# Scores of the first attention: four 64-row matmuls a tile become two of 128 rows

## The chip, the cores and the metric

The kernel runs on one core of one Trainium2 chip. The metric is the device time of one execution in microseconds (us); the time before is the median of three executions that were not profiled. In the profile PE is the matmul engine and PEld its weight load, DVE the vector engine, ACT the scalar engine, POOL GpSimd, and SP the engine that issues most of the plain transfers.

## The reference

Two graph attention layers over 12,500 nodes and 200,000 edges sorted by target node, four heads of 64 channels each, every layer followed by layer norms. The change lies in the scores of the first one:

```python
Q = (enh @ Wq + bq).reshape(N, H, D)
K = (enh @ Wk + bk).reshape(N, H, D)
mod_k = K[src] + 0.2 * rel[:, None, :]
scores = jnp.einsum('ehd,ehd->eh', Q[dst], mod_k) / D ** 0.5
seg_max = jax.ops.segment_max(scores, dst, num_segments=N)
ex = jnp.exp(scores - seg_max[dst])
...
agg = jax.ops.segment_sum(w[:, :, None] * V[src], dst, num_segments=N)
```

Everything is float32.

## The kernel before, in words

Four stages follow one another. `make_tables` builds index and mask tables. `project_nodes` (tag `qkv`) takes the nodes in 98 blocks of 128, computes queries, keys and values, and writes keys and values to a table `kv` in HBM and the scaled queries, transposed, to `qt`. `attend_typed` (tag `typed`) is the first attention, `attend_plain` (tag `plain`) the second.

Both attentions cut the edges into 521 tiles of 384 and work on a window of 32 consecutive target nodes for each tile (`TN`); a tile also looks at the first 32 edges of the next, so it has 416 score columns. For every head the 32 query vectors of the window are multiplied with all 416 keys; a mask (`far`) then throws away the pairs that are no edge.

One tile of `attend_typed`, by engine:

- POOL (`gather`, L766) issues three indirect DMAs, each of 128 rows of `kv`, into one of eight row slots. It waits until the aggregation of the tile eight before has freed the slot.
- PE: `relate` (L843, L844) forms the relation vectors, `arrive` (L852) turns the key part of the rows into columns, `turn_weights` (L860, L861) turns the softmax weights of an earlier tile, `aggregate` (L889) multiplies these with the values of a still earlier tile in 16 matmuls of 32 output rows, and `score` (L875) forms the scores.
- DVE: `lower_bound` (L997) masks the scores and takes their maximum, `prepare` (L986) makes the relation matrix, `add_keys` (L969, L970) adds keys and relation vectors into `kt`.
- ACT: `weigh` (L1167) the exponential, besides copies out of PSUM; `put` (L1174) copies an aggregate.
- SP: `put_out` (L812) stores the result of a tile eight back, then `fetch` (L786) loads the queries of this tile; `fetch_kinds`, `fetch_match` and `fetch_index` follow in some tiles.

The order on each engine is written out by hand: `interleave` calls the parts of a step in a fixed order, each with a lag. On PE a step is turn_weights (lag 5), aggregate (6), score (3), relate (0), arrive (1). `score(t)` waits for the query transfer of its tile (semaphore `q_in`), for `add_keys` of tile t+1 (`kt_ready`) and for `lower_bound` of tile t-1 (`max_ready`). `lower_bound(t)` on DVE waits for `score(t)`, and `add_keys` stands behind it in DVE's order. So a loop runs from the scores over DVE back to the next scores. Besides the tiles there are 98 blocks of finished nodes, whose output projection and layer norms are put between the tiles (`update` and `move` on PE, `sum_up`, `normalize`, `vary`, `end_norm` and `join` on DVE).

In `score`, head h = 0 to 3 has the queries of the window in rows 64*(h%2) to 64*(h%2)+63 of the tile `q`, at pair h//2, and its output in PSUM rows 32h to 32h+31 of `p_s`:

```python
last = pe.matmul(p_s[at:at + TN, 0:SLOTS], q[own, m, :, h // 2], kt[own, h // 2, lo:lo + SLOTS],
                 start=True, stop=True, tile_position=(HC * (h % 2), at), skip_group_check=True)
```

So each of the four matmuls takes a block of 64 rows by 32 columns of PE's array, and the four blocks overlap neither in columns nor, of neighbouring heads, in rows. Every float32 matmul shows in the profile as two weight loads and two matmul records.

Of the kernel before, what the change touches and what calls it, by code (L numbers as in the profile page):

```python
# [14 lines left out]
P = 128  # L15
# [3 lines left out]
HEADS = 4  # L19
# [49 lines left out]
C_ID = 0  # L69
C_NEG1 = C_ID + P  # L70
C_LATER = C_NEG1 + P
C_KEY1 = C_LATER + 1
C_COVER = C_KEY1 + 2
C_THIN = C_COVER + PER
# [11 lines left out]
C_CMP1 = C_PASS + G_PASSES  # L86
C_N = C_CMP1 + 2
FAR = float(2.0 ** 50)
# [12 lines left out]
def constants():  # L101

    c = np.zeros((P, C_N), np.float32)
    p = np.arange(P)
    c[:, C_ID:C_ID + P] = np.eye(P)
    c[:, C_DIAG:C_DIAG + TN] = p[:, None] % TN == np.arange(TN)
    c[:G_GT, C_THR:C_THR + TPB] = TN * (G_GT * np.arange(TPB)[None, :] + np.arange(G_GT)[:, None])
    c[:REL, C_CMP] = np.arange(REL)
    c[REL:REL + TN, C_CMP] = np.arange(TN)
    c[REL:REL + TN, C_CMP + 1] = 1.0  # L110
    c[REL:REL + TN, C_NEG:C_NEG + P] = -BIG * (np.arange(TN)[:, None] == p[None, :] % TN)
    c[:, C_TAU:C_TAU + TPB] = p[:, None] // TN == np.arange(TPB)
    c[:, C_GRP:C_GRP + TPB] = P * p[:, None] + TN * np.arange(TPB)
    c[:, C_SLOT:C_SLOT + G_LEFT] = np.arange(G_LEFT)
    c[:, C_PASS:C_PASS + G_PASSES] = G_MAIN * np.arange(G_PASSES)
    c[:TN, C_CMP1:C_CMP1 + 2] = c[REL:REL + TN, C_CMP:C_CMP + 2]
    c[:TN, C_NEG1:C_NEG1 + P] = c[REL:REL + TN, C_NEG:C_NEG + P]
    c[1:, C_LATER] = 1.0
    c[:TN, C_KEY1] = 1 + np.arange(TN)
    c[:TN, C_KEY1 + 1] = 1.0  # L120
    c[:, C_TYPE] = p % REL
    c[:, C_CODE] = -FAR * (1 + p % TN)
    cover, thin = np.zeros(TROWS * PER), np.full(TROWS * PER, -1.0)
    for b in range(ROWS):
        if settled_tiles(b) <= TILES:
            cover[settled_tiles(b)] = min(P * (b + 1), N)
    thin[0:TILES - 2] = TN
    c[:TROWS, C_COVER:C_COVER + PER] = cover.reshape(TROWS, PER)
    c[:TROWS, C_THIN:C_THIN + PER] = thin.reshape(TROWS, PER)
    return c  # L130
# [221 lines left out]
class Kernel:  # L352


    def __init__(self, nc, ctx, inputs, out, flag):
# [8 lines left out]
        self.match = dram("match", (2, TROWS * PER, SLOTS), U8)  # L364
        self.qt = dram("qt", (P, NP, 2))
        self.kv = dram("kv", (NP, KV))
# [148 lines left out]
def project_nodes(k):  # L515
# [4 lines left out]
    with Stage(nc, "qkv") as z:  # L520
# [8 lines left out]
        kv = z.sb("kv", [P, AHEAD, KV])  # L529
        q_now = z.sb("q_now", [P, AHEAD, P, 2])  # L530
        beta = z.sb("beta", [P, D])
# [6 lines left out]
        (x_turned, x_t_ready, q_done, q_ready, kv_done, kv_ready, setup, spread_ready, bias_done, bias_ready, settled2, kept,  # L538
         zero_ready, zero_out) = (z.sem(n) for n in (
            "x_turned", "x_t_ready", "q_done", "q_ready", "kv_done", "kv_ready", "setup", "spread_ready", "bias_done", "bias_ready",  # L540
            "settled2", "kept", "zero_ready", "zero_out"))
        block = z.block()
# [3 lines left out]
        def _(sp):  # L546
# [19 lines left out]
            def store(t):  # L566
                b = t.slot(AHEAD)
                sp.wait_ge(kv_ready, t.n + 1)
                sp.dma_start(k.kv[bass.ds(t.n * P, P), :], kv[:, b]).then_inc(kv_out[b], 16)
                sp.wait_ge(q_ready, t.n + 1)  # L570
                sp.dma_start(k.qt[:, bass.ds(t.n * P, P)].rearrange("p n a -> p (n a)"),
                             q_now[:, b].rearrange("p n a -> p (n a)")).then_inc(q_out[b], 16)

# [73 lines left out]
        def _(act):  # L647
# [6 lines left out]
            def queries(t):  # L654
# [4 lines left out]
                for pair in range(2):  # L659
                    last = act.activation(q_now[:, o, :, pair], p_q[:, t.slot(2), pair * P:pair * P + P],  # L660
                                          ACT.Identity, bias=bq[:, pair:pair + 1], scale=scale)
# [17 lines left out]
def attend_typed(k):  # L679
# [9 lines left out]
    with Stage(nc, "typed") as z:  # L689
# [7 lines left out]
        rel = z.sb("rel", [P, 2, MAIN])  # L697
        q = z.sb("q", [P, M, TN, 2])
        kt = z.sb("kt", [P, 2, 4 * MAIN + SPILL])
# [73 lines left out]
        def _(sp):  # L773
# [6 lines left out]
            def fetch(t):  # L780
                m = t.slot(M)
                node = first_nodes(k, sp, t, places)
                if not t.known_below(M):
                    sp.wait_ge(scores_ready, t.n - M + 1)
                    sp.sem_inc(slot_free, 1)
                sp.dma_start(q[:, m], k.qt[:, bass.ds(node, TN)]).then_inc(q_in[m], 16)  # L786
                g, group = group_of(t)
# [50 lines left out]
        def _(pe):  # L838
# [24 lines left out]
            def score(t):  # L863
                m = t.slot(M)
                pe.wait_ge(q_in[m], t.use(M) * 16 + 16)
                if not (isinstance(t.q, int) and t.n == TILES - 1):
# [4 lines left out]
                lo = t.slot(4) * MAIN  # L871
                for h in range(HEADS):
                    at = TN * h
                    own = slice(HC * (h % 2), HC * (h % 2) + HC)
                    last = pe.matmul(p_s[at:at + TN, 0:SLOTS], q[own, m, :, h // 2], kt[own, h // 2, lo:lo + SLOTS],  # L875
                                     start=True, stop=True, tile_position=(HC * (h % 2), at), skip_group_check=True)
                last.then_inc(scores_ready, 1)
# [82 lines left out]
        def _(v):  # L960
# [127 lines left out]
            init(v.memset(row1[:], 1.0))  # L1088
            for to in (p_w, result, bias_o, bias_1, ones, message, message_t, x1, x1_t):
                init(v.memset(to[:], 0.0))  # L1090
# [1857 lines left out]
```

## Time and profile before

| what | before |
|---|---|
| time, median of 3 (lowest to highest) | 4468.4 us (4467.4 to 4470.13) |
| the profiled execution's own time: its span | 6181.0 us |
| PE, DVE, POOL, ACT busy, share of the span | 69%, 53%, 49%, 42% |
| busy of L875 (scores), 4168 records | 835.7 us |
| busy of L766 and L1298 (gathers), 1563 each | 1491.3 us and 1486.0 us |

The profiled execution takes 38% longer than the ones that were timed. Busy times and orders are of the profiled execution; what bounds the timed one has to be read with that in mind. Matmuls are pipelined and their ends are modelled, so the starts are what can be trusted.

### The profile page before, as it was taken

Reading aid. Unit: us, or ns where it says so; the run is one execution under the profiler, and the core shown is the slowest. Engines: PE = TensorE matmul, PEld = TensorE weight load, DVE = VectorE, ACT = ScalarE, POOL = GpSimd, SP = SyncE. Lnnn points to the kernel's source line nnn. Section 1 sums busy time; section 2 is a strip of 40 time slices with the busy share of each in tenths; the row PEclk is TensorE's granted clock in tenths of the full one; section 3 lists DMA queues with packets and bytes.
Section 4 is the critical chain, followed back from the end, with each engine's and each line's share of the span. In section 5 each row is a group of like instructions: output and inputs, shape, how many; then the busy total and the mean of one; then the engine's idle time right before and its main releaser. Section 6 shows DMA issues by size and latency. Waiting matters only on the chain. (4 is left out here: it accounts for less than half of the span.)

```text
span 6181.0 us, 164556 instructions
## 1 busy us (share of the span) xinstructions
PE 4261.5 (69%) x50798; PEld 2746.6 (44%) x50798; DVE 3295.8 (53%) x10527; ACT 2576.2 (42%) x6781; POOL 3049.7 (49%) x3229
## 2 busy tenths in 40 slices
PE   7958878777778787778786555555555555555554
PEld 4634444444444444444443444444444443444443
DVE  3235555555555555555554455555555555555555
ACT  2323344444444444444343444444444444444444
POOL 1245555545555555555452555555555555555553
PEclk9989999999999999999997666656566566565666
DMA  7856676666666666666664555555555555555554
GB/s 224 282 163 191 185 189 186 186 186 185 186 187 183 186 186 187 185 186 186 184 185 114 145 153 156 152 151 153 152 153 153 150 152 149 154 152 152 154 150 123
DMA packets 820553, 1055.91 MB, mean 171 GB/s; under 512 B 458633, under 2 KB 632338, under 8 KB 820464
## 3 DMA queue, kind: packets, MB, share of 16 engines
q0 software_dynamic: 225072, 730.03, 42.9%
q1 hardware_dynamic: 594078, 324.02, 20.6%
q10 hardware_dynamic: 1314, 0.99, 0.1%
q14 instruction: 73, 0.60, 0.0%
q8 instruction: 16, 0.26, 0.0%
HBM read 919.46 MB, written 133.59 MB: 170 GB/s over the span
## 5 line engine op out<-in xcount | busy, mean ns | idle before, releaser
L766 POOL DMA_INDIRECT typed_rows<-kv,typed_index x1563 | 1491.3, 954 | 1470.8 <-remote 570.5
L1298 POOL DMA_INDIRECT plain_rows<-xp,plain_index x1563 | 1486.0, 951 | 1359.5 <-remote 536.1
L875 PE MATMUL typed_p_s<-typed_kt,typed_q 64*32 64x416 f32 x4168 | 835.7, 549 | 336.6 <-issue 289.7
L997 DVE CUSTOM_DVE_ANT_0 typed_weight<-typed_p_s,typed_far 128x416 f32<-128x416 f32 x521 | 308.3, 592 | 1113.6 <-PE typed_p_s L875 1080.8
L1400 PE MATMUL plain_p_o<-plain_rows,plain_weight_t 128*32 128x65 f32 x16672 | 630.5, 296 | 331.5 <-issue 310.7
L1433 DVE SCALAR_TENSOR_TENSOR plain_p_s<-plain_p_s,plain_a_dst,plain_damped 128x416 f32<-128x416 f32 x521 | 342.3, 657 | 865.9 <-ACT plain_damped L1553 475.1
L1389 PE MATMUL plain_p_s<-all_cst,plain_rows 128*128 128x128 f32 x2084 | 546.2, 395 | 346.0 <-issue 319.6
L1375 PE MATMUL plain_p_w<-all_cst,plain_weight 128*128 128x128 f32 x1563 | 437.5, 404 | 431.6 <-issue 286.0
L1400 PEld LDWEIGHTS plain_p_o<-plain_rows,plain_weight_t 128*32 128x32 f32 x16672 | 459.2, 154 | 556.6 <-issue 516.7
L1167 ACT ACTIVATE typed_weight<-typed_weight,typed_col 128x416 f32<-128x416 f32 x521 | 334.7, 642 | 806.6 <-issue 549.7
L1389 PEld LDWEIGHTS plain_p_s<-all_cst,plain_rows 128*128 128x128 f32 x2084 | 406.0, 210 | 463.6 <-issue 437.6
L889 PE MATMUL typed_p_o<-typed_rows,typed_weight_t 128*32 128x65 f32 x16672 | 421.3, 227 | 247.3 <-issue 147.7
L1553 ACT ACTIVATE plain_damped<-plain_p_s,plain_a_dst 128x416 f32<-128x416 f32 x521 | 312.9, 601 | 503.1 <-DMA plain_a_dst<-xp 267.7
L970 DVE TENSOR_TENSOR typed_kt<-typed_p_kt,typed_rel 128x768 f32<-128x768 f32 x521 | 495.2, 950 | 46.8 <-remote 16.7
L875 PEld LDWEIGHTS typed_p_s<-typed_kt,typed_q 64*32 64x32 f32 x4168 | 169.4, 107 | 722.1 <-issue 705.7
L852 PE MATMUL typed_p_kt<-all_cst,typed_rows 128*128 128x128 f32 x3126 | 480.5, 295 | 11.5 <-DMA typed_rows<-kv,typed_index 6.3
L1375 PEld LDWEIGHTS plain_p_w<-all_cst,plain_weight 128*128 128x128 f32 x1563 | 240.2, 196 | 531.0 <-issue 380.0
L852 PEld LDWEIGHTS typed_p_kt<-all_cst,typed_rows 128*128 128x128 f32 x3126 | 422.0, 155 | 74.7 <-issue 21.0
L889 PEld LDWEIGHTS typed_p_o<-typed_rows,typed_weight_t 128*32 128x32 f32 x16672 | 293.5, 112 | 343.7 <-issue 232.2
L1560 ACT ACTIVATE plain_weight<-plain_alpha,plain_col 128x416 f32<-128x416 f32 x521 | 332.8, 639 | 244.1 <-issue 125.6
L1576 ACT COPY plain_result<-plain_col 128x1 f32<-128x1 f32 x521 | 97.9, 188 | 763.0 <-remote 760.1
L1174 ACT COPY typed_result<-typed_p_o 128x65 f32<-128x65 f32 x521 | 111.6, 214 | 725.4 <-remote 547.6
(191 smaller groups left out, 6936.5 us busy)
## 6 DMA issues: line engine op xcount, KB each, us to landing
typed_match<-match SPq DMA_DIRECT2D x131, 208.0 KB
plain_match<-match SPq DMA_DIRECT2D x131, 208.0 KB
agg<-qkv_zero SPq DMA_DIRECT2D x98, 264.0 KB
typed_agg<-agg SPq DMA_DIRECT2D x98, 264.0 KB
plain_agg<-agg SPq DMA_DIRECT2D x98, 264.0 KB
kv<-qkv_kv SPq DMA_DIRECT2D x98, 258.0 KB
typed_kinds<-match SPq DMA_DIRECT2D x131, 192.0 KB
typed_rows<-kv,typed_index POOLq DMA_INDIRECT x1563
```

What stands on the lines that cost most here:

```text
L766: pool.indirect_dma_start(rows[:, r, j, :], None, k.kv, bass.IndirectOffsetOnAxis(ap=index[:, g, at:at + 1], axis=0)).then_inc(rows_in[r], 16)
L852: last = pe.transpose(p_kt[:, pair, j * P:j * P + P], rows[:, t.slot(R), j, pair * P:pair * P + P], ident)
L875: last = pe.matmul(p_s[at:at + TN, 0:SLOTS], q[own, m, :, h // 2], kt[own, h // 2, lo:lo + SLOTS], start=True, stop=True, tile_position=(H ...
L889: last = pe.matmul(p_o[at:at + TN, 0:V], weight_t[:, t.slot(2), j * P + at:j * P + at + TN], v[:, D + V * h:D + V * h + V], start=j == 0, ...
L970: v.tensor_tensor(kt[:, :, lo:lo + MAIN], p_kt[:, :, 0:MAIN], both_pairs(0, MAIN), ALU.add).then_inc(kt_ready, 1)
L1167: act.activation(weight[:, c], weight[:, c], ACT.Exp, bias=col[:, t.slot(4), LOW:LOW + 1]).then_inc(exp_done, 1)
L1298: pool.indirect_dma_start(rows[:, r, j, :], None, k.xp, bass.IndirectOffsetOnAxis(ap=index[:, g, at:at + 1], axis=0)).then_inc(rows_in[r], 16)
L1375: pe.transpose(p_w[:, t.slot(2), j * P:j * P + P], weight[:, t.slot(2), j * P:j * P + P], ident)
L1389: last = pe.transpose(p_s[:, c, j * P:j * P + P], a_src[:, A_SRC:A_DST], ident)
L1400: last = pe.matmul(p_o[at:at + TN, t.slot(2), 0:V], weight_t[:, t.slot(2), j * P + at:j * P + at + TN], val[:, V * h:V * h + V], start=j = ...
L1433: v.scalar_tensor_tensor(p_s[:, c, 0:SLOTS], p_s[:, c, 0:SLOTS], a_dst[:, m, 0:1], damped[:, c], ALU.add, ALU.max).then_inc(leaked, 1)
L1560: act.activation(weight[:, c], alpha[:, c], ACT.Exp, bias=col[:, t.slot(4), LOW:LOW + 1]).then_inc(exp_done, 1)
```

## The change

The two heads of a pair are scored by one matmul. The query tile of a pair becomes 128 rows by 64 columns: head 2*pair in rows 0 to 63 of columns 0 to 31, head 2*pair+1 in rows 64 to 127 of columns 32 to 63, and zeros in the two other corners. The zeros are written once, before the first tile. The queries are loaded by two transfers, one for each half of the rows, and lie in HBM with the pair ahead of the node (`qt` is (128, 2, nodes) in place of (128, nodes, 2)). Constants that only the start reads are moved behind the part of the constants that stays in SBUF.

```diff
-        self.qt = dram("qt", (P, NP, 2))
+        self.qt = dram("qt", (P, 2, NP))
...
-        q_now = z.sb("q_now", [P, AHEAD, P, 2])
+        q_now = z.sb("q_now", [P, AHEAD, 2, P])
...
                 sp.wait_ge(q_ready, t.n + 1)
-                sp.dma_start(k.qt[:, bass.ds(t.n * P, P)].rearrange("p n a -> p (n a)"),
-                             q_now[:, b].rearrange("p n a -> p (n a)")).then_inc(q_out[b], 16)
+                sp.sem_inc(q_seen, 1)
+                sp.dma_start(k.qt[:, :, bass.ds(t.n * P, P)], q_now[:, b]).then_inc(q_out[b], 16)
...
-                    last = act.activation(q_now[:, o, :, pair], p_q[:, t.slot(2), pair * P:pair * P + P],
+                    last = act.activation(q_now[:, o, pair], p_q[:, t.slot(2), pair * P:pair * P + P],
...
-        q = z.sb("q", [P, M, TN, 2])
+        q = z.sb("q", [P, M, 2, 2 * TN])
...
-                sp.dma_start(q[:, m], k.qt[:, bass.ds(node, TN)]).then_inc(q_in[m], 16)
+                for y in range(2):
+                    own = slice(HC * y, HC * y + HC)
+                    sp.dma_start(q[own, m, :, TN * y:TN * y + TN], k.qt[own, :, bass.ds(node, TN)]).then_inc(q_in[m], 16)
...
-                pe.wait_ge(q_in[m], t.use(M) * 16 + 16)
+                pe.wait_ge(q_in[m], t.use(M) * 32 + 32)
...
-                for h in range(HEADS):
-                    at = TN * h
-                    own = slice(HC * (h % 2), HC * (h % 2) + HC)
-                    last = pe.matmul(p_s[at:at + TN, 0:SLOTS], q[own, m, :, h // 2], kt[own, h // 2, lo:lo + SLOTS],
-                                     start=True, stop=True, tile_position=(HC * (h % 2), at), skip_group_check=True)
+                for pair in range(2):
+                    at = HC * pair
+                    last = pe.matmul(p_s[at:at + HC, 0:SLOTS], q[:, m, pair], kt[:, pair, lo:lo + SLOTS],
+                                     start=True, stop=True, tile_position=(0, at), skip_group_check=True)
...
-            for to in (p_w, result, bias_o, bias_1, ones, message, message_t, x1, x1_t):
+            for to in (p_w, result, bias_o, bias_1, ones, message, message_t, x1, x1_t, q):
                 init(v.memset(to[:], 0.0))
```

On PE, one step of the steady order in `attend_typed`, before:

```order
L861 MATMUL typed_p_w<-all_cst,typed_weight 32x128
L889 MATMUL typed_p_o<-typed_rows,typed_weight_t 32x65 x16
L875 MATMUL typed_p_s<-typed_kt,typed_q 32x416 x4
L843 MATMUL typed_p_r<-typed_hit,typed_rel_a 128x384
L844 MATMUL typed_p_r<-typed_hit,typed_rel_b 128x384
L852 MATMUL typed_p_kt<-all_cst,typed_rows 128x128 x6
```

and now:

```order
L860 MATMUL typed_p_w<-all_cst,typed_weight 32x128
L887 MATMUL typed_p_o<-typed_rows,typed_weight_t 32x65 x16
L873 MATMUL typed_p_s<-typed_kt,typed_q 64x416 x2
L842 MATMUL typed_p_r<-typed_hit,typed_rel_a 128x384
L843 MATMUL typed_p_r<-typed_hit,typed_rel_b 128x384
L851 MATMUL typed_p_kt<-all_cst,typed_rows 128x128 x6
```

The order stays; four score matmuls of 32 output rows have become two of 64.

On SP, two steps of the loop of `attend_typed`, before:

```order
L812 ISA
L812 DMA agg<-typed_result 4x32x66
L786 ISA
L786 DMA typed_q<-qt 128x64
L805 DMA typed_match<-match 128x1664
L778 DMA typed_index<-all_idx 128x12
L317 TENSOR_LOAD all_first_row
```

and now:

```order
L811 ISA
L811 DMA agg<-typed_result 4x32x66
L785 REGISTER_ALU
L785 DMA typed_q<-qt 64x2x32
L785 ISA
L785 DMA typed_q<-qt 64x2x32
L804 DMA typed_match<-match 128x1664
L775 DMA typed_index<-all_idx 128x12
L314 TENSOR_LOAD all_first_row
```

A second query transfer, with an address computation of its own, stands ahead of the other transfers of the step.

## Rows read from the trace of the kernel before

**Rows 1.** Three stages: busy PE, PEld, DVE, ACT, POOL; then PEclk, DMA share, GB/s.
```profile
0.00:350.00 350.00, 288.66 (x1400) 186.24 (x1400) 109.72 (x296) 101.52 (x296) 72.39 (x103) 0.97 0.75 239
350.00:3297.00 2947.00, 2337.76 (x28347) 1369.87 (x28351) 1651.19 (x4588) 1178.82 (x2941) 1491.33 (x1563) 0.94 0.69 185
3297.00:6181.00 2884.00, 1635.07 (x21062) 1190.45 (x21055) 1534.87 (x5646) 1295.91 (x3544) 1485.96 (x1563) 0.61 0.57 148
```
**Rows 2.** The page's group of gathers: count | busy us, mean ns | idle before.
```profile
L766 POOL DMA_INDIRECT typed_rows<-kv,typed_index x1563 | 1491.3, 954 | 1470.8 <-remote 570.5
```
**Rows 3.** Timeline of POOL: first and last gathers (start, duration, [idle before]).
```profile
350.72 1.09 POOL L766 DMA_INDIRECT typed_rows<-kv,typed_index  x1 [33.33 <-DVEq L1134]
353.36 0.95 POOL L766 DMA_INDIRECT typed_rows<-kv,typed_index  x1 [0.30 <-issue]
...
3278.58 0.95 POOL L766 DMA_INDIRECT typed_rows<-kv,typed_index  x1 [0.30 <-issue]
3359.56 0.94 POOL L1298 DMA_INDIRECT plain_rows<-xp,plain_index  x1 [80.03 <-DMA plain_index<-all_idx]
...
6124.04 0.95 POOL L1298 DMA_INDIRECT plain_rows<-xp,plain_index  x1 [0.30 <-issue]
```
**Rows 4.** Timeline of a slow tile: aggregation, scores, and the copy that waits for aggregation.
```profile
1804.25 0.66 PE L889 MATMUL typed_p_o<-typed_rows,typed_weight_t 128*32 128x65 f32 x32
1805.15 1.15 PE L875 MATMUL typed_p_s<-typed_kt,typed_q 64*32 64x416 f32 x3 [0.24 <-issue]
1807.24 0.96 PE L875 MATMUL typed_p_s<-typed_kt,typed_q 64*32 64x416 f32 x5 [0.94 <-issue]
1807.55 0.21 ACT L1174 COPY typed_result<-typed_p_o 128x65 f32<-128x65 f32 x1 [1.69 <-remote]
1808.13 0.34 PE L843 MATMUL typed_p_r<-typed_hit,typed_rel_a 128*128 128x384 bf16 x1
```
**Rows 5.** Timeline of a quick tile, from its aggregation to the next scores.
```profile
1660.74 0.66 PE L889 MATMUL typed_p_o<-typed_rows,typed_weight_t 128*32 128x65 f32 x32 [1.13 <-ACT typed_message_t L1178]
1661.36 0.90 PE L875 MATMUL typed_p_s<-typed_kt,typed_q 64*32 64x416 f32 x8
1662.19 0.34 PE L843 MATMUL typed_p_r<-typed_hit,typed_rel_a 128*128 128x384 bf16 x1
1662.50 0.59 DVE L997 CUSTOM_DVE_ANT_0 typed_weight<-typed_p_s,typed_far 128x416 f32<-128x416 f32 x1 [3.72 <-PE typed_p_s L875]
1662.53 0.82 PE L852 MATMUL typed_p_kt<-all_cst,typed_rows 128*128 128x128 f32 x6
1663.18 0.49 PE L860 MATMUL typed_p_w<-all_cst,typed_weight 128*128 128x128 f32 x3
1663.71 0.95 DVE L970 TENSOR_TENSOR typed_kt<-typed_p_kt,typed_rel 128x768 f32<-128x768 f32 x1
1665.07 0.51 PE L875 MATMUL typed_p_s<-typed_kt,typed_q 64*32 64x416 f32 x1 [0.49 <-DVE typed_kt L970]
```
**Rows 6.** Timeline of the second attention: two steps of DVE that follow directly.
```profile
4703.76 0.22 DVE L1514 SCALAR_TENSOR_TENSOR plain_square<-plain_rstd,plain_half 128x1 f32<-128x1 f32 x1 [0.78 <-DVE plain_rstd L1515]
4705.31 0.16 DVE L1515 SCALAR_TENSOR_TENSOR plain_rstd<-plain_square,plain_rstd 128x1 f32<-128x1 f32 x1 [1.32 <-DVE plain_square L1514]
```
**Rows 7.** SP: a query transfer and the next one issued; then a row of its waits.
```profile
1667.99 0.34 SPq L786 DMA_DIRECT2D typed_q<-qt  x1
1668.64 0.33 SPq L805 DMA_DIRECT2D typed_match<-match  x1
...
SPq L785 <- PE typed_p_s L875: 920.5, 431, 9.8
```
**Rows 8.** DMA: packets by queue (q1 is SP's and ACT's), the 40 slices' rates.
```profile
GB/s 224 282 163 191 185 189 186 186 186 185 186 187 183 186 186 187 185 186 186 184 185 114 145 153 156 152 151 153 152 153 153 150 152 149 154 152 152 154 150 123
...
q1 hardware_dynamic: 594078, 324.02, 20.6%
```
**Rows 9.** DVE's clears at the start of the first attention.
```profile
L1090 DVE MEMSET typed_p_w<- 128x512 f32 x1 | 0.5, 485 | 0.1
```

More of the change, by code:

```diff
@@ L69 @@
 C_ID = 0
[L70 to L73, printed above, removed]
+C_LATER = C_ID + P
+C_COVER = C_LATER + 1
 C_THIN = C_COVER + PER
@@ L86 @@
 C_CMP1 = C_PASS + G_PASSES
-C_N = C_CMP1 + 2
+C_NEG1 = C_CMP1 + 2
+C_N = C_NEG1 + P
 FAR = float(2.0 ** 50)
@@ L118, in constants @@
     c[1:, C_LATER] = 1.0
-    c[:TN, C_KEY1] = 1 + np.arange(TN)
-    c[:TN, C_KEY1 + 1] = 1.0
     c[:, C_TYPE] = p % REL
@@ L538, in project_nodes @@
         (x_turned, x_t_ready, q_done, q_ready, kv_done, kv_ready, setup, spread_ready, bias_done, bias_ready, settled2, kept,
-         zero_ready, zero_out) = (z.sem(n) for n in (
+         zero_ready, zero_out, q_seen) = (z.sem(n) for n in (
             "x_turned", "x_t_ready", "q_done", "q_ready", "kv_done", "kv_ready", "setup", "spread_ready", "bias_done", "bias_ready",
-            "settled2", "kept", "zero_ready", "zero_out"))
+            "settled2", "kept", "zero_ready", "zero_out", "q_seen"))
         block = z.block()
```

## The prediction

> **What bounds the kernel now.** I read the stages first, then the order of time in single tiles. By stage, the profiled execution spends 350 us on tables and projection, 2947 us on the first attention and 2884 us on the second [rows 1]. Only the middle one is changed in its loop. PE is its busiest engine (2338 of 2947 us), and the scores are its largest group. That makes the change look large. Two things speak against reading it so.
>
> First, the profiled execution takes 6181 us, the end of the third stage [rows 1], and the timed ones 4468.4. 1713 us of what the profile shows are therefore not in the time. Where they lie can be seen in single tiles. In a slow one, the 32 records of the aggregation start at 1804.25, but the copy that waits for their end starts only at 1807.55, and the eight score records straggle in two lots until the next group starts at 1808.13: 3.88 us for 40 matmul records [rows 4]. In a quick one the same 40 records take from 1660.74 to 1662.19, 1.45 us, and the scores 0.83 of it [rows 5]. No semaphore explains the 2.4 us between the two; the profile calls the waits "issue" or "remote". The same happens on DVE in the other attention: a step of 0.22 us that started at 4703.76 lets the next one, which needs nothing else, start at 4705.31 [rows 6]. I read these as stalls of the recording, that is, as not in the timed runs. Then the tile to look at is the quick one.
>
> Second, POOL alone explains the time. A gather is issued every 0.95 + 0.30 = 1.25 us when nothing holds POOL [rows 3], so three of them make 3.75 us a tile, and 521 tiles 1954 us, in either attention (1563 gathers each [rows 1]). With 351 us before the first gather, 81 between the last of the first attention and the first of the second, and 57 after the last [rows 3], that is 351 + 1954 + 81 + 1954 + 57 = 4397 us, 98.4% of 4468.4. In the profile POOL sits idle for 1471 us of the first attention [rows 2]: it waits for slots that the stalled PE frees late.
>
> The quick tile also shows the loop behind POOL's. Scores start at 1661.36, DVE's masking of them at 1662.50, the key addition at 1663.71, and the next scores, which waited for it, at 1665.07 [rows 5]: 3.71 us, just under POOL's 3.75. PE's own work in this tile, 1.45 us plus 1.52 us from 1662.19 to the next aggregation (to 1663.71, where it starts beside the key addition), is 2.97 us. So PE's throughput does not bind; only the time from the start of the scores to their end lies in a loop, and that loop is level with POOL.
>
> **The scores.** Four matmuls become two. What matters is how many follow one another. Six records of 128 columns run from 1662.53 to 1663.18 [rows 5], 0.11 us each, so 416 columns take 0.35 us. Eight records one after the other would be 2.8 us; they take 0.83 [rows 5], so the four blocks run together, in two rounds (one for each record of a matmul). The 32 records of the aggregation, in four column blocks of 128 rows, also run together: 1660.74 to 1661.36 for 32 is 0.02 us each, where 65 columns at the rate above take 0.055. The new matmuls are two column blocks of 128 rows and need two rounds as well, if they run together like the aggregation's. The term is 0. Its ends: two blocks in turn, four rounds, +0.70 us a tile; or the gap that is left in the 0.83 us beside two rounds of 0.35 falls away, -0.13. I take 0 since the aggregation, on whole rows, is the nearest row. At 521 tiles the ends are +365 and -68 us, if nothing hides them.
>
> The Trainium skill (TensorEngine Tiling (Array Packing), Restrictions and Gotchas) says that row tiles cannot access the same PSUM bank at once. The four blocks here do write one bank, from two row halves, and by that rule the old scores would need four rounds and the change would save two. The quick tile does not bear it out.
>
> **The query transfers.** SP issues one more DMA in each of 521 tiles. From one query DMA to the next DMA is 0.65 us [rows 7], which I take for it, 339 us of SP's time in all. SP stood waiting 920 us for scores in the profile [rows 7] and fetches queries four tiles ahead, so I cost it at nothing; the transfers queued behind it (masks, indices, results) are ahead of need too. If that cover is gone, +0.65 us in the tiles where SP is late.
>
> The bytes stay. Packets double from 128 of 256 bytes to 256 of 128 bytes a tile. The mean packet of SP's queue takes 20.6% of 16 engines' 6181 us over 594,078 packets [rows 8], 34 ns, so 128 more are at most 128 x 34 / 16 = 0.27 us of the 16 engines a tile (141 us in all); at no cost for a smaller packet, 0. I take 0.1, nearer the lower end as the mean packet is 545 bytes, and hide it under POOL's pace: 0 on the path.
>
> **The rest.** The store of the queries has twice the packets, of half the size: at the same 34 ns, 98 x 128 x 34 / 16 = 27 us at most, against 0 if PE hides it as it should (289 of 350 us busy [rows 1]); I take 1. Clearing the query tile (512 columns) costs 0.5 us once [rows 9]. The activation that writes the queries without a stride is off the path.
>
> **Sum.** 4468.4 + 0 + 0 + 1 + 0.5 = 4470 us. In the profiled execution I expect a smaller span all the same: 4 of 52 matmul records a tile fall away, and a slow tile that spends 3.88 / 40 = 0.1 us on each would give back 0.4 us: up to 210 us in 521 tiles, and 150 as an estimate, since not every tile is slow. The sum against 6181 is then about 6030, and these 150 us are not in the timed median, as 1713 others were not.
>
> **The rivals.**
>
> *PE's stalls are real.* If the slow tile is also what the timed runs have, the change gives back the same 0.4 us in each of them: 4468 - 150 = 4320, with less if fewer tiles are slow. For it: nothing in the trace names the recording as the cause. Against it: 2947 us for the first attention leave 4468 - 350 - 2947 = 1171 for the second, 2.25 us a tile, under the 2.85 us of three gathers' busy time alone. Chance 0.15.
>
> *The old scores take four rounds in the timed runs*, the two row halves in turn. Then two rounds of 0.35 us a tile are saved, 365 us in all, but no more than down to POOL's floor of 4397. The quick tile's 0.83 us for all eight records speaks against it [rows 5]. Chance 0.03. This is what the rule on banks, quoted above, would give.
>
> *The DMA engines become the bound; slower.* The first attention moves 185 GB/s in 5.66 us a tile [rows 1], 1.05 MB; in the 4 us that a tile of the timed run has, that is 262 GB/s, and the highest slice of the profile, with large packets, shows 282 [rows 8]. If the engines are full, each added packet counts: 0.1 to 0.27 us a tile, 4520 to 4610, and 4550 at 0.16. It decides from the point where a gather lands after PE asks for its rows. Against it: POOL's floor explains the time without it. Chance 0.18.
>
> *SP falls behind; slower.* A tile in four also carries masks and indices; 0.65 us lost in these 130 is 85 us, 4553. SP's 920 us of waiting in the profile speak against it, though they come from stalled tiles. Chance 0.08.
>
> *The two column blocks run in turn.* The loop becomes 3.71 + 0.70 = 4.41 us, 0.66 over POOL's pace: 4468 + 344 = 4812. The aggregation's rows speak against it. Chance 0.07.
>
> **How the numbers follow.** The forecast, no change, has 0.49. Its own range is 4460 to 4480. The range takes in the two slower rivals of DMA and SP up to 4560, which is most of them, and below reaches 4400, the floor that POOL sets and a mild form of the first rival: left out are the column blocks in turn (0.07), the full form of the first rival (some 0.08) and the far end of the DMA rival (0.04). Faster by over 0.2% (about what a measurement of this kernel can tell from no change) has 0.15 + 0.03 = 0.18, slower by as much 0.18 + 0.08 + 0.07 = 0.33.
>
> **What would show it.** Right: in the trace after, four score records in quick tiles, in two pairs that start together, with 0.7 to 0.85 us from the first to the relation matmul; quick tiles of 3.7 us; fewer slow tiles and a span near 6030 beside an unchanged median. Wrong: 1.4 us or more for the scores in quick tiles (blocks in turn), rows that PE waits for (DMA), query waits on PE (SP), or a median that falls with the span (real stalls).

## The result, and the profile after

The change makes the kernel slower.

| what | before | after |
|---|---|---|
| time, median (lowest to highest) | 4469.26 us (4467.4 to 4472.05, 4 runs) | 4632.98 us (4627.01 to 4640.0, 4 runs) |
| ratio, with 95% interval | | 1.0367 (1.0352 to 1.0381) |
| the profiled execution's span | 6181.0, and 4466.9 in a second one | 4625.3 us |
| busy of the scores (L875, now L873) | 835.7, and 471.6 in the second | 495.6 us |

The profile of before that the prediction was read from was 38% longer than the runs. The same kernel was therefore profiled once more (the first run below), and that execution has the length of the timed ones. What is compared here is that second profile with the one of after.

First the stages of after, as in [rows 1]: the first attention from its first to its last gather, then the second one. Columns: busy PE, PEld, DVE, ACT, POOL, then the granted clock, the DMA share and GB/s.

```profile
350.00:2529.00 2179.00, 1844.75 (x26051) 1227.37 (x26050) 1624.87 (x4547) 1125.58 (x2918) 1503.22 (x1563) 0.97 0.87 250
2607.00:4571.00 1964.00, 1252.12 (x20622) 943.40 (x20623) 1445.14 (x5343) 1247.50 (x3399) 1487.94 (x1563) 0.77 0.79 214
```

The same two stages in the second profile of the kernel before:

```profile
350.00:2371.00 2021.00, 1787.34 (x28116) 1176.27 (x28118) 1613.20 (x4547) 1122.74 (x2918) 1495.77 (x1562) 1.00 0.91 269
2450.00:4413.00 1963.00, 1259.38 (x20638) 950.62 (x20642) 1443.92 (x5342) 1246.27 (x3399) 1487.10 (x1563) 0.76 0.80 214
```

The second attention is the same to 1 us. The first one takes 2179 us instead of 2021: 158 us more, which is the whole loss. None of the listed engines has become much busier (PE 57 us, PEld 51, DVE 12, ACT 3, POOL 7), and the DMA engines are less full than before (0.87 against 0.91). So all of them wait more, for something that is not in this table: SP, whose work is to issue transfers.

SP's waits in this stage in the second profile of before (engine, line, waited for: us in total, times, longest):

```profile
SPq L785 <- PE typed_p_s L875: 439.5, 296, 11.7
SPq L818 <- DVE typed_message L1011: 107.8, 53, 2.5
SPq L817 <- DVE typed_message L1011: 20.7, 9, 2.6
```

and after:

```profile
SPq L782 <- PE typed_p_s L873: 26.8, 28, 8.0
SPq L817 <- DMA agg<-typed_result: 2.8, 9, 0.5
SPq L817 <- DVE typed_message L1009: 2.4, 5, 0.6
SPq L816 <- DVE typed_message L1009: 1.9, 3, 0.8
```

Of 568 us of waiting in the first attention 34 are left. Without them SP works 2021 - 568 = 1453 us before, 2.79 a tile, and 2179 - 34 = 2145 us after, 4.12 a tile. A tile took 3.88 (2021 / 521). On the average SP now needs longer for a tile than the whole tile took before, and has become the bound. That shows on the other engines as late transfers. In the page of after the relation matrix on DVE (L984) waits 131.5 us for the kinds, a wait that the second profile of before does not have. The group that answers to [rows 2] is the one of L763; its 708 us of idle time stand against 559.0 in the second profile of before. The page of after (two queues, then groups as in [rows 2]):

```profile
q1 hardware_dynamic: 681646, 323.99, 27.8%
q14 instruction: 209, 1.71, 0.1%
...
L763 POOL DMA_INDIRECT typed_rows<-kv,typed_index x1563 | 1504.2, 962 | 708.4 <-issue 422.7
...
L873 PE MATMUL typed_p_s<-typed_kt,typed_q 128*64 128x416 f32 x2084 | 495.6, 550 | 308.3 <-issue 249.8
...
L984 DVE TENSOR_SCALAR typed_hit<-typed_kinds,all_cst 128x384 bf16<-128x384 uint8 x521 | 231.6, 445 | 138.4 <-DMA typed_kinds<-match 131.5
```

Where SP's time went shows in its timeline (start, duration, operation; x2 means two transfers in a row). Before, second profile:

```profile
1626.42 0.39 SPq L818 DMA_DIRECT2D typed_agg<-agg  x1
1627.57 0.63 SPq L812 DMA_DIRECT2D agg<-typed_result  x1
...
1635.32 0.34 SPq L786 DMA_DIRECT2D typed_q<-qt  x1
1635.97 0.33 SPq L805 DMA_DIRECT2D typed_match<-match  x1
...
1642.73 0.39 SPq L818 DMA_DIRECT2D typed_agg<-agg  x1
1643.46 0.64 SPq L812 DMA_DIRECT2D agg<-typed_result  x1
```

After:

```profile
1643.69 0.40 SPq L817 DMA_DIRECT2D typed_agg<-agg  x1
1647.81 0.70 SPq L811 DMA_DIRECT2D agg<-typed_result  x1
...
1656.21 1.34 SPq L785 DMA_DIRECT2D typed_q<-qt  x2
1657.82 0.37 SPq L804 DMA_DIRECT2D typed_match<-match  x1
...
1711.55 0.40 SPq L817 DMA_DIRECT2D typed_agg<-agg  x1
1715.60 0.71 SPq L811 DMA_DIRECT2D agg<-typed_result  x1
```

Two things are longer. From the query transfer to the next one, before took 1635.97 - 1635.32 = 0.65 us, the same as in [rows 7]; after takes 1657.82 - 1656.21 = 1.61, 0.96 us more; the same in each of 521 tiles would be 500 us (over all tiles of the loop that are followed by this transfer the medians are 0.60 and 1.60). And once in 16 tiles, at the end of a turn of SP's loop, a step that takes 0.73 us elsewhere (1642.73 to 1643.46) takes 4.12 (1643.69 to 1647.81, and again at 1711.55). Before, the same place costs 1.15 (1626.42 to 1627.57). The 27 turns (tiles 89 to 520) have 119 us of this step after and 31 before, 89 us more, or 3.3 a turn. It is the jump back that is long: where SP enters the loop for the first time the step takes 0.82 us after and 0.84 before, at the 26 returns 4.05 to 5.13 after and 1.15 before. Together these are 589 of the 692 us by which SP's work grew. The remaining 100 are not broken down further; part of them are stores that take 0.70 instead of 0.63 us.

The loss does not lie in all tiles. The first 89 are written out ahead of the loop, the other 432 run in its 27 turns of 16. Cut at the gather of tile 89 (columns as in [rows 1]), before in the second profile, then after:

```profile
350.00:686.70 336.70, 295.48 (x4538) 190.86 (x4540) 244.09 (x667) 172.21 (x408) 255.34 (x267) 0.97 0.90 265
686.70:2371.00 1684.30, 1491.86 (x23583) 985.41 (x23586) 1369.11 (x3881) 950.53 (x2511) 1240.43 (x1295) 1.00 0.92 270
```

```profile
349.60:687.50 337.90, 297.82 (x4188) 195.33 (x4187) 242.50 (x663) 172.06 (x407) 254.44 (x267) 0.97 0.90 263
687.50:2529.00 1841.50, 1547.33 (x21866) 1032.04 (x21864) 1382.37 (x3885) 953.52 (x2511) 1249.12 (x1296) 0.97 0.86 247
```

The 89 tiles have the second transfer too and take 338 us instead of 337: SP's waiting there falls from 122 to 25 us and still covers it. The whole loss, 157 us, lies in the loop, 5.8 us a turn. There SP waited 446 us before, 16.5 a turn, and waits 9 after, in all turns together. The second transfers want 16 x 0.96 = 15.4 us of a turn, nearly all of that cover, and the end of the turn 3.3 more. DVE's wait for the kinds has the same shape: 127 of its 131.5 us lie in the loop, and 79 of them in the fourth tile of a turn, which needs the first kinds that SP issues after the turn's end (at 1650.64 in the turn above):

```profile
1656.57 0.42 DVE L984 TENSOR_SCALAR typed_hit<-typed_kinds,all_cst 128x384 bf16<-128x384 uint8 x1 [3.38 <-DMA typed_kinds<-match]
```

### The profile page after: what moved, and what is told of

Its sections match the earlier page's. It is cut to its first block and busy times, and to the rows that moved or that the text cites. A ratio compares the mean times of both kernels' runs of the same rounds, so it can differ in the third digit from the quotient of the medians.

```text
span 4625.3 us, 162050 instructions
## 1 busy us (share of the span) xinstructions
PE 3447.8 (75%) x48714; PEld 2396.9 (52%) x48714; DVE 3269.0 (71%) x10528; ACT 2519.7 (54%) x6781; POOL 3065.3 (66%) x3229
## 3 DMA queue, kind: packets, MB, share of 16 engines
q1 hardware_dynamic: 681646, 323.99, 27.8%
q14 instruction: 209, 1.71, 0.1%
## 5 line engine op out<-in xcount | busy, mean ns | idle before, releaser
L763 POOL DMA_INDIRECT typed_rows<-kv,typed_index x1563 | 1504.2, 962 | 708.4 <-issue 422.7
L1387 PEld LDWEIGHTS plain_p_s<-all_cst,plain_rows 128*128 128x128 f32 x2084 | 346.0, 179 | 754.9 <-issue 733.4
L873 PE MATMUL typed_p_s<-typed_kt,typed_q 128*64 128x416 f32 x2084 | 495.6, 550 | 308.3 <-issue 249.8
L1373 PE MATMUL plain_p_w<-all_cst,plain_weight 128*128 128x128 f32 x1563 | 373.3, 362 | 105.1 <-ACT plain_weight L1558 97.4
L1398 PE MATMUL plain_p_o<-plain_rows,plain_weight_t 128*32 128x65 f32 x16672 | 446.8, 265 | 0.6 <-DVE plain_weight_t L1426 0.6
L1398 PEld LDWEIGHTS plain_p_o<-plain_rows,plain_weight_t 128*32 128x32 f32 x16672 | 344.8, 136 | 95.7 <-issue 62.7
L1437 DVE CUSTOM_DVE_ANT_0 plain_alpha<-plain_p_s,plain_far 128x416 f32<-128x416 f32 x521 | 308.4, 592 | 97.7 <-issue 43.7
L887 PE MATMUL typed_p_o<-typed_rows,typed_weight_t 128*32 128x65 f32 x16672 | 349.9, 225 | 17.8 <-ACT typed_message_t L1176 16.3
L1542 ACT ACTIVATE plain_far<-plain_match,all_cst 128x416 bf16<-128x416 uint8 x521 | 333.9, 641 | 9.2 <-DMA plain_match<-match 9.2
L1145 ACT ACTIVATE typed_far<-typed_match,all_cst 128x416 bf16<-128x416 uint8 x521 | 333.9, 641 | 0.0
L984 DVE TENSOR_SCALAR typed_hit<-typed_kinds,all_cst 128x384 bf16<-128x384 uint8 x521 | 231.6, 445 | 138.4 <-DMA typed_kinds<-match 131.5
```

The lines of the kernel that those rows point to most:

```text
L763: pool.indirect_dma_start(rows[:, r, j, :], None, k.kv, bass.IndirectOffsetOnAxis(ap=index[:, g, at:at + 1], axis=0)).then_inc(rows_in[r], 16)
L873: last = pe.matmul(p_s[at:at + HC, 0:SLOTS], q[:, m, pair], kt[:, pair, lo:lo + SLOTS], start=True, stop=True, tile_position=(0, at), skip ...
L887: last = pe.matmul(p_o[at:at + TN, 0:V], weight_t[:, t.slot(2), j * P + at:j * P + at + TN], v[:, D + V * h:D + V * h + V], start=j == 0, ...
L1373: pe.transpose(p_w[:, t.slot(2), j * P:j * P + P], weight[:, t.slot(2), j * P:j * P + P], ident)
L1387: last = pe.transpose(p_s[:, c, j * P:j * P + P], a_src[:, A_SRC:A_DST], ident)
L1398: last = pe.matmul(p_o[at:at + TN, t.slot(2), 0:V], weight_t[:, t.slot(2), j * P + at:j * P + at + TN], val[:, V * h:V * h + V], start=j = ...
```

## Experiments

Each run is named by its label; the times are medians, the ratios are to the kernel before on the same chip, with 95% intervals. "SP's wait" is its wait for the scores, 439.5 us before and 26.8 after.

**The kernel before, profiled again.** No edit.

> The kernel before, unchanged, profiled once more, since its first profile took 38% longer than its timed runs. If the stalls of that profile belong to the recording of that one execution, this one shows a span of about 4470 us, first-attention tiles of 3.87 us in place of 5.63 and few slow tiles; if every profile of this kernel is stretched, about 6180 again. SP theory: SP waits for scores for at least 200 us in the first attention, so it has some slack, but less than the 920 us of the first profile.

4473.1 us, ratio 0.9999 (0.9988 to 1.0009), span 4466.9 us. The 1713 us by which the first profile was longer do not come back: they belonged to that one execution. So did half of SP's 920 us of waiting in [rows 7]: here it is 439.5. The quick tile of the prediction was the right one to look at.

**e1: the matmuls alone.** The two matmuls of the change, on the old query tile with its one transfer.

```diff
-                for h in range(HEADS):
...
+                for pair in range(2):
+                    at = HC * pair
+                    last = pe.matmul(p_s[at:at + HC, 0:SLOTS], q[:, m].rearrange("p n a -> p (n a)"), kt[:, pair, lo:lo + SLOTS],
+                                     start=True, stop=True, tile_position=(0, at), skip_group_check=True)
```

> The two 128-row matmuls of the change, but the query tile is loaded as before, by one transfer of 128 x 256 bytes into 64 columns; both pairs are multiplied with the same 64 columns, so the corners of zeros and the right scores are left out. SP theory (the second transfer makes SP the bound): 4469 us, within 15 of before. PE theory (the new matmuls are slower): about 4630, all of the loss. DMA theory (more small packets): 4469.

4469.84 us, ratio 0.9992 (0.9982 to 1.0001). The matmuls are worth nothing, and cost nothing:

```profile
SPq L785 <- PE typed_p_s L874: 438.1, 300, 11.7
```

**e2: the transfers alone.** The matmuls of before, the query transfer cut into two halves of 64 rows, each row still 256 contiguous bytes.

```diff
-                sp.dma_start(q[:, m], k.qt[:, bass.ds(node, TN)]).then_inc(q_in[m], 16)
+                for y in range(2):
+                    own = slice(HC * y, HC * y + HC)
+                    sp.dma_start(q[own, m], k.qt[own, bass.ds(node, TN)]).then_inc(q_in[m], 16)
```

> The four matmuls of before; only the query transfer is split in two, 64 rows each, still 256 bytes a row, so the packets are as before. SP theory: slower, 4500 to 4640 (one more issue of some 0.35 to 0.55 us and its address work in every tile, and the longer loop on SP). PE theory and DMA theory: 4469.

4602.62 us, ratio 1.0291 (1.0274 to 1.0309). 130 of the 164 us come with the second issue alone. The bytes and the rows' packets stay; what the queue has more is 8336 packets of 4 bytes, 16 for each added issue (602,414 packets instead of 594,078). The row of the issue (shortest, median and longest, ns) and SP's wait:

```profile
L788 SPq DMA_DIRECT2D typed_q<-qt x1042: 246/507/1119, 350.6 to 2505.2; - x174
```

```profile
SPq L785 <- PE typed_p_s L877: 48.2, 77, 8.5
```

**e3: one transfer for the change.** The zeros lie in HBM too: `qt` has four blocks (pair, head of the pair), and one transfer of 128 x 4 x 32 fills the whole query tile.

```diff
-        self.qt = dram("qt", (P, 2, NP))
+        self.qt = dram("qt", (P, 4, NP))
...
+                sp.dma_start(q[:, m], k.qt[:, :, bass.ds(node, TN)]).then_inc(q_in[m], 16)
```

> The change with its zeros kept in HBM: the whole query tile, zeros included, comes by one transfer of 128 x 4 x 128 bytes, 512 packets and twice the bytes. SP theory: most of the loss comes back, 4470 to 4520. PE theory: 4630. DMA theory: slower than the change, over 4640, since the packets double once more.

4513.65 us, ratio 1.0087 (1.0070 to 1.0104): most of the loss is gone, although this transfer has 512 packets of 128 bytes, twice those of the change. Of the 40 us that are left, 24 lie ahead of the first gather (374.2 us instead of 350.1), where four activations write the queries instead of two and their store has twice the bytes (which of the two costs them is not shown); the first attention takes 3.92 us a tile. SP's wait is 290.1 us.

**e4: a longer loop.** The kernel before with four increments of an idle semaphore on SP in each tile.

```diff
+                for _ in range(4):
+                    sp.sem_inc(padding, 1)
```

> The kernel before with four counts of a spare semaphore behind each query transfer on SP: no transfer is added, only instructions, so that SP's loop of 16 tiles grows by 64. Throughput theory (SP has some 550 us of waiting in the first attention of before, and the change uses up all of it): SP loses about 0.26 us a tile, 135 us, and at most 100 more if the 3.7 us stall at each turn of the loop appears; both fit in the waiting, so 4474 to 4500 us. Stall theory (the 26 stalls of 3.7 us at the loop's turn cause the loss): 4560 or more if the stall appears.

4467.8 us, ratio 0.9996 (0.9986 to 1.0006). SP's wait falls to 334.2 us, and nothing is lost: as long as SP waits, its work is free. The end of its loop's turn did not become longer here, so this run says nothing of that stall.

**e5: the second half issued by ACT.** The change, but each half has its own queue.

```diff
+                act.dma_start(q[HC:P, m, :, TN:2 * TN], k.qt[HC:P, :, bass.ds(node, TN)]).then_inc(q_in2[m], 16)
```

> The change, but the second query transfer of each tile is issued by ACT, with the packets, the zeros and the matmuls of the change. Throughput theory: most of the loss comes back, 4470 to 4500, and SP again waits for scores for 300 us or more. If the loss came from the packets or the DMA engines: 4620 to 4640.

4523.3 us, ratio 1.0120 (1.0104 to 1.0137). SP is relieved (wait 330.5 us), but ACT seems to pay: its copy of the relation vectors, which follows the new issue in ACT's order, now stands 156.3 us behind "issue", a wait that the second profile of before does not have.

```profile
ACT typed_rel L1163 <- issue: 156.3, 418, 0.7
```

**e6: masks first.** The change, with the kinds and masks issued ahead of the tile's queries instead of behind them, since DVE's wait for the kinds was the visible one.

```diff
-                if not t.known_below(M):
-                    sp.wait_ge(scores_ready, t.n - M + 1)
...
                     fetch_match((g + 1) % 2, bass.ds(t.n + 1, TPB))
+                if not t.known_below(M):
+                    sp.wait_ge(scores_ready, t.n - M + 1)
```

> The change with SP's order turned: the transfers of kinds and masks are issued ahead of the two query transfers of the same step. Throughput theory: no help, 4610 to 4640, and another wait takes the place of DVE's 131 us for kinds. Order theory (SP keeps up, but the kinds stand behind the longer query transfers): 4480 to 4520.

4637.78 us, ratio 1.0380 (1.0363 to 1.0397): no help, and DVE waits as long for the kinds as in the change (139.3 us). The order on SP is not what is lacking; that its time is, fits.

**e8: SP relieved in the kernel before.** Kinds and masks (two transfers in four tiles) are issued by ACT.

```diff
+                act.dma_start(kinds[:, slot], k.match[0, at, 0:MAIN].unsqueeze(0).broadcast_to((P, TPB, MAIN))).then_inc(kinds_in[slot], 16)
...
+                act.dma_start(match[:, slot], k.match[1, at].unsqueeze(0).broadcast_to((P, TPB, SLOTS))).then_inc(match_in[slot], 16)
```

> The kernel before with the transfers of kinds and masks moved from SP to ACT. Throughput theory: SP is not the bound before the change, so its relief gives little, 4440 to 4475; if SP's lateness in single tiles already costs the first attention its 3.88 us against POOL's 3.75, up to 65 us come back, 4410.

4490.01 us, ratio 1.0047 (1.0030 to 1.0064). SP's wait rises to 575.4 us and the kernel becomes 20 us slower: before the change SP was not the bound. That the 20 us are ACT's added issues is likely, but no row here isolates it.

**e9: one tiny transfer more.** The kernel before with a second issue in each tile, of 4 bytes.

```diff
+                sp.dma_start(tiny[0:1, m:m + 1], k.first[0:1].rearrange("(o n) -> o n", o=1)).then_inc(tiny_in[m], 16)
```

> The kernel before, with one more transfer of 4 bytes per tile issued on SP just behind the tile's query transfer (66 issues in a turn of SP's loop instead of 50, as the changed kernel has), whose bytes nobody reads. Throughput theory (SP must issue everything of a tile in less than the 3.88 us that POOL, DVE and PE take; its work is about 2.8 us per tile of 521): one more issue of 0.3 to 0.6 us gives 3.1 to 3.5 us of SP per tile, still hidden: 4469 to 4495, SP's wait for the scores falls from 440 us to 130 to 290 us. If the number of issues per loop turn is what makes the stall of 3.5 us at SP's loop end, that stall shows here too (26 turns, about 95 us in sum), and SP's wait falls by it as well, to 40 to 190 us; if the stall alone, not SP's total, cost the time of the change, then about 4560. If the stall depends on the shape of the transfers, not on their number, it stays at 0.3 us per turn.

4471.45 us, ratio 1.0002 (0.9992 to 1.0012). As many issues as the change, the added ones of 0.29 us, and no loss; the wait falls to 278.9. The stall at the loop's end does not appear: the number of transfers does not make it.

```profile
L791 SPq DMA_DIRECT2D typed_tiny<-first x521: 239/287/627, 349.9 to 2373.4; - x174
```

```profile
SPq L787 <- PE typed_p_s L882: 278.9, 292, 9.6
```

**e10: SP's time alone.** As e4, with 16 increments: no transfer more than before.

```diff
+                for _ in range(16):
+                    sp.sem_inc(padding, 1)
```

> The kernel before, with 16 increments of a semaphore that nobody waits for on SP behind each query transfer, some 1.0 us per tile and no DMA more. Throughput theory: SP's work becomes about 3.8 us per tile, as much as the tile takes, SP's wait for the scores falls from 440 us to under 60 us, and the time rises to between 4480 and 4560; half of the change's loss or more without any of its transfers. Rival (the loss lies in the transfers themselves: their packets, their landing): no change, 4466 to 4473.

4603.89 us, ratio 1.0302 (1.0284 to 1.0319), more than the 4560 expected. From the query transfer to the next issue SP now takes 1.53 us (0.65 before), and the instruction queue shows that the stall at the loop's end is there as well: this is its row on the page, 73 packets before and 209 after.

```profile
1660.71 0.35 SPq L787 DMA_DIRECT2D typed_q<-qt  x1
1662.24 0.33 SPq L808 DMA_DIRECT2D typed_match<-match  x1
```

```profile
q14 instruction: 242, 1.98, 0.1%
```

```profile
SPq L786 <- PE typed_p_s L878: 36.4, 46, 7.8
```

This is the loss of e2 (4602.62) without a transfer added, and with no packet more in SP's queue (594,078); only the instruction queue has grown. What counts is SP's time: the increments in each tile and the stall at the end of a turn, which this run has together. Here too the 89 tiles ahead of the loop lose next to nothing (339 us instead of 337).

**e11: the packets alone.** The change's layout and matmuls, but one transfer of 128 x 2 x 32 in place of two of 64 x 2 x 32, so the same 256 packets of 128 bytes in one issue. The second head's queries are not in their own corner.

```diff
-                for y in range(2):
-                    own = slice(HC * y, HC * y + HC)
-                    sp.dma_start(q[own, m, :, TN * y:TN * y + TN], k.qt[own, :, bass.ds(node, TN)]).then_inc(q_in[m], 16)
+                sp.dma_start(q[:, m, :, 0:TN], k.qt[:, :, bass.ds(node, TN)]).then_inc(q_in[m], 16)
```

> The changed kernel's layout of the queries and its two 128-row matmuls, but one transfer of all 128 rows, 32 columns of each pair (the same packets of 128 bytes as the changed kernel's two transfers, 256 of them). Left out: the second head's queries do not go to their own corner, and the zeros are not in their place, so the scores are others. Throughput theory (what counts is SP's time of issuing): one issue of 0.4 to 0.6 us, SP's wait for the scores 250 to 430 us, 4468 to 4495. Rival (the loss lies in the twice as many, half as long packets): as the changed kernel, about 4630.

4486.45 us, ratio 1.0036 (1.0022 to 1.0050). The packets, with an issue that is itself 0.27 us longer, cost 16 us of 164.

```profile
L783 SPq DMA_DIRECT2D typed_q<-qt x521: 500/610/637, 349.3 to 2388.8; - x174
```

```profile
SPq L782 <- PE typed_p_s L871: 304.8, 291, 10.2
```

**e12: SP relieved in the changed kernel.** The edit of e8, made in the kernel after.

> The changed kernel, with the transfers of the kinds and the masks (two per four tiles) issued by ACT instead of SP. SP then issues 58 transfers in a turn of its loop instead of 66. Throughput theory: SP loses 0.22 us of issuing per tile (and its loop-end stall of 0.185 us per tile, if the program of a turn is now short enough), so its wait for the scores rises from 27 us to 150 us or more, and the first attention goes from 4.185 to 3.90 to 3.98 us per tile: 4480 to 4530, where the same move made the kernel before slower by 20 us. If the stall stays, 4520 to 4560. Rival (the loss is the later landing or the number of the query's packets): about 4630, or 4650 with ACT's own cost.

4498.26 us, ratio 1.0068 (1.0051 to 1.0085). The move that made the kernel before 20 us slower takes some 135 of the change's 164 us away. SP's wait is back at 139.3 us, and the stall at the loop's end is gone with 8 transfers fewer in a turn (80 packets of instructions). The same edit has opposite signs on the two kernels, as it must if SP bounds only the second. It shortens SP's work and takes the stall away at once, so it does not say which of the two gives back how much.

```profile
SPq L783 <- PE typed_p_s L856: 139.3, 208, 8.6
```

```profile
q14 instruction: 80, 0.65, 0.0%
```

Put side by side by SP's wait for the scores, the runs fall into two groups.

| run | SP's wait, us | time, us |
|---|---|---|
| e8 | 575.4 | 4490.0 |
| before | 439.5 | 4473.1 |
| e1 | 438.1 | 4469.8 |
| e4 | 334.2 | 4467.8 |
| e5 | 330.5 | 4523.3 |
| e11 | 304.8 | 4486.5 |
| e3 | 290.1 | 4513.7 |
| e9 | 278.9 | 4471.5 |
| e12 | 139.3 | 4498.3 |
| e2 | 48.2 | 4602.6 |
| e10 | 36.4 | 4603.9 |
| after | 26.8 | 4633.0 |
| e6 | 17.8 | 4637.8 |

Down to 279 us of waiting nothing need be lost; a run that loses above that has a reason of its own (ACT's issues in e5 and e8, the projection in e3, the small packets or their longer issue in e3 and e11). Below 50 us each added piece of SP work is paid. The four runs below 50 us are also the four that have the stall at the loop's end, so the table alone can't tell SP's work in the tiles from the stall. No run beats the kernel before: the part of the change that could have gained, the matmuls, is worth nothing by itself (e1).

## Why the prediction was wrong

It forecast 4470 us, no change, in a range of 4400 to 4560, and gave slower 0.33. The time is 4633, outside of the range.

*The step that failed* is that of the query transfers on SP: "SP stood waiting 920 us for scores in the profile [rows 7] ... so I cost it at nothing". Three things in it were wrong.

- The cover was half as large. The 920 us came from the stretched execution. The prediction discarded that profile's 1713 us for PE and POOL and named the doubt for SP only in a rival ("though they come from stalled tiles"). Read with the same discount, the cover would have been an unknown between nothing and 920 us. It is 1.09 us a tile (568 us in 521 tiles, 440 of them for the scores).
- The price was too small. One more transfer was put at 0.65 us, the distance of the old one to the next. Measured in the same way the pair takes 1.61, so 0.96 more: two issues of 0.57 us (median of 1042) in place of one of 0.34. Half the rows did not make an issue shorter but longer: 0.51 us for 64 contiguous rows in e2.
- The stall at the end of SP's loop was not thought of: some 3.3 us in each of 27 turns.

With 0.96 instead of 0.65 us and the 89 us of stalls, 589 us stand against 568 of waiting, and the forecast would have been "slower, by little". The 100 us more that SP's work grew by make up most of the rest: 692 - 568 = 124, and 34 of waiting that stay, are the 158.

*The rival "SP falls behind"* had the right mechanism at 0.08. Its price, "0.65 us lost in these 130 is 85 us, 4553", was mis-sized: it is not 0.65 us in one tile in four, but in the loop 5.8 us a turn, since there SP's throughput over the whole turn decides and its lag comes out where the kinds are needed. That fits e6, where kinds and masks went first and nothing was gained.

*Right:* The scores' term of 0. After, a tile has four records, as forecast, and the relation matmul follows 0.85 us after their start, 0.83 in [rows 5]:

```profile
1601.64 0.92 PE L873 MATMUL typed_p_s<-typed_kt,typed_q 128*64 128x416 f32 x4 [0.37 <-issue]
1602.49 0.34 PE L842 MATMUL typed_p_r<-typed_hit,typed_rel_a 128*128 128x384 bf16 x1
```

So neither rival on the matmuls holds: not the blocks in turn (4812), not the four rounds of before. Both forms take the same time to 0.02 us, which also speaks once more against the rule on banks that the prediction quotes from the Trainium skill.

*Right:* that the stretched profile's stalls are not in the timed runs (the rival at 4320 falls with the second profile), and POOL's floor: the second attention takes 1963 us against the 1954 worked out from [rows 3]. The first one took 2021 before, 67 more, so POOL alone does not set its pace. The span that was forecast for the profile after, near 6030, did not come (4625.3): the stretching was no property of the kernel.

*Right in its bound:* the DMA engines. The term was 0 to 141 us, taken as 0; e11 shows 16 us, of which the longer issue may be a part. The queue's 87,568 packets more (681,646 after, 594,078 in [rows 8]) are not what costs the rest; the prediction's 128 more a tile left out the 16 of 4 bytes that the second issue brings (e2). The rival that made them the bound (0.18) falls: the engines are less busy after than before.

*"What would show it"* named "query waits on PE (SP)" as the wrong sign for SP. It did not come, and yet SP was at fault: the queries are fetched so early that in the loop they still land 8.4 us before their scores start (median; 9.9 before), and the profile names nobody who waits for them. What SP delivers late is what it fetches with less lead, the kinds (131.5 us on DVE). PE's "issue" ahead of the scores grew as well (249.8 us against 164.8); what it waits for there is not shown.

A rule against the change was there to be weighed. The rows show that halves of a transfer cost as much issue time each as the whole, or more. The Trainium skill (DMA: Bandwidth & Descriptors, Rules for kernel authors) advises against two transfers to disjoint partition halves and for one of 128 partitions, because both halves are spread over the same engines. The advice is borne out here; its reason is not the one that cost time, which was the issue on SP (e10 loses as much as e2 without a transfer more). The Trainium skill (Perfetto Trace Analysis, What "DMA-bound" means) lists the sequencer of the issuing engine as a bound of its own, and there the trace of the loop agrees (9 us of waiting in 1841).

What stays open: about 100 us by which SP's work grew beside the two causes named, the last 8 to 16 us that the 128-byte packets seem to cost (e11; e12 against e8), and how much of the loss the loop's stall makes alone, since no run has the change's two issues on SP without it except e12, which moves other work too. An estimate: SP bounds the loop, so without the stall's 3.3 us of the 5.8 that a turn has lost, 2.5 us a turn would stay, 68 of the 157 us.

## What to carry to other kernels

An engine that only issues transfers has a throughput like any other, and the table of busy times doesn't list it: add up what it issues in a step, start to start, and compare with the step, before a transfer is split. Waiting time is cover only as far as it is there in an execution of normal length; where a profile is longer than the timed runs, the waits of every engine are to be discounted, also those that argue for one's own forecast. An edit in a long unrolled loop can add a stall at its end that no single instruction shows. Where some steps are written out ahead of the loop, compare them and the loop's turns apart: here one change cost nothing in the first and everything in the second.

## What the runs showed of the hardware

- The time that SP takes to issue a transfer goes with its shape; neither bytes nor packets order it. Medians: 0.34 us for 128 rows of 256 contiguous bytes, 0.51 for 64 such rows (e2), 0.57 for 64 x 2 x 32 (after; 0.61 in e5, where it stands alone), 0.61 both for 128 x 2 x 32 (e11, 256 packets) and for 128 x 4 x 32 (e3, 512 packets), 0.29 for 4 bytes (e9).
- The end of a turn of SP's loop costs 3.3 us more in four of the kernels. It comes with fetches: the instruction queue has 73 to 81 packets in the runs without the stall, and 205 to 242 in those with it (e2, e6, e10, after). The 1.11 MB more of after (1.71 against 0.60) would be 43 KB at each of the 26 returns; the first entry, which needs no jump back, is not longer (0.82 us). Sixteen more increments a tile bring it (e10); four (e4) and a tiny transfer (e9) don't. Neither the count of SP's recorded instructions in a turn decides it (302 in e2 and after, which have it; 318 in e4, which doesn't) nor that of transfers (66 in after; 66 in e9, which doesn't have it). The Trainium skill (Runtime: NRT & Kernel Launch, Instruction fetch mechanics) says that a taken branch whose target lies outside the two pages that an engine holds must fetch the page first, before it goes on. The packets and the short first entry agree with it; no run here measured where the limit lies.
- One profiled execution of an unchanged kernel was 38% longer than the next one (6181.0 and 4466.9 us), with gaps such as those in [rows 4] and [rows 6].
